# Attention with values of the narrow column groups multiplied in pairs, and a third buffer of probabilities

## The reference

```python
q, k, v = (to_heads(q), to_heads(k), to_heads(v))
dots = jnp.einsum('bhid,bhjd->bhij', q * scale, k)
causal = jnp.triu(jnp.ones((n, n), bool), k=1)
dots = jnp.where(causal, MASK_VAL, dots)
attn = jax.nn.softmax(dots, axis=-1)
out = jnp.einsum('bhij,bhjd->bhid', attn, v)
out = out.transpose(0, 2, 1, 3).reshape(b, n, d)
return out @ Wo.T + bo
```

```python
counts = jnp.bincount(a_e, length=E)
keep = counts <= cap
valid = keep[a_e]
```

## Time and profile before

| | |
|---|---|
| median of 3 runs | 1375.12 us (1373.54 to 1376.57) |
| profiled execution | 1374.71 us, span 1373.0 us |
| TensorE busy | 1273.9 us, 93% |
| VectorE busy | 1093.9 us, 80% |
| ScalarE busy | 942.2 us, 69% |
| GpSimd busy | 397.3 us, 29% |
| middle batch, 539.8 to 700.2 us | 160.4 us |
| granted TensorE clock, mean | 0.979 (1.00 from 120 to 1120 us) |
| DMA | 95.18 MB, mean 69 GB/s |

### The profile page before, as it was taken

One profiled execution on the slowest core, in us unless ns is written; L12 is line 12 of the kernel. 1 busy time (PEld: TensorE's weight loads), 2 busy tenths in 40 slices (PEclk: granted clock), 3 DMA queues, 4 the chain that ended last, 5 costly groups with the idle time before them and its releaser, 6 DMA issues.

```text
span 1373.0 us, 25088 instructions
## 1 busy us (share of the span) xinstructions
PE 1273.9 (93%) x8693; PEld 600.0 (44%) x8693; DVE 1093.9 (80%) x3527; ACT 942.2 (69%) x1697; POOL 397.3 (29%) x508
## 2 busy tenths in 40 slices
PE   6899999999999999999999999999999999999884
PEld 4433334444454444454444444544445544444332
DVE  6888888778887888878887788878888788779634
ACT  2257777777767777767767777677777677676752
POOL 3223322333232322332323332323222323222111
PEclk9889999999999999999999999999999999999977
DMA  4580443543325443324435423254442243340001
GB/s 134 114 156 13 70 70 58 100 75 74 68 37 100 90 70 70 61 63 89 70 59 101 83 62 68 40 101 89 70 70 53 38 92 70 58 69 32 1 1 34
DMA packets 57832, 95.18 MB, mean 69 GB/s; under 512 B 8352, under 2 KB 51488, under 8 KB 51744
## 3 DMA queue, kind: packets, MB, share of 16 engines
q1 hardware_dynamic: 55664, 92.30, 35.7%
q10 hardware_dynamic: 2032, 1.19, 0.3%
HBM read 59.91 MB, written 33.55 MB: 68 GB/s over the span
## 4 chain that ended last, share of the span: by engine, by line
PE 61%; DVE 21%; ACT 6%; issue 3%; DVEq 3%; DMA 2%; POOL 1%; SPq 1%; ACTq 0%; POOLq 0%
PE o_bank L1319 15%; PE s L1300 14%; PE st L1285 12%; DVE s L1011 8%; PE misc L1202 6%; PE misc L1186 4%; PE misc L1194 4%; DVE max_full L1015 3%; ACT probs L860 3%; PE misc L543 3%; DVE xn L519 2%; ACT q_stack L847 2%; DVEq L1022 2%; DVE stats L510 1%; DVE o_tok L1108 1%
## 5 line engine op out<-in xcount | busy, mean ns | idle before, releaser
L860 ACT ACTIVATE probs<-st 128x512 f32<-128x512 f32 (+1 forms) x1216 | 632.5, 581 | 192.2 <-PE st L1285 119.0
L1011 DVE CUSTOM_DVE_ANT_0 s<-s,causal 128x128 f32<-128x128 f32 (+3 forms) x1024 | 493.4, 502 | 131.9 <-PE s L1300 127.2
L1300 PE MATMUL s<-k_stack,q_stack 96*128 96x512 bf16 (+3 forms) x1536 | 493.7, 332 | 33.1 <-DVE max_full L1015 13.4
L1285 PE MATMUL st<-q_stack,k_stack 108*128 108x512 bf16 (+3 forms) x1536 | 486.8, 331 | 11.7 <-ACT probs L860 11.2
L1015 DVE TENSOR_REDUCE max_full<-s 128x1 f32<-128x512 f32 x512 | 349.7, 683 | 46.6 <-PE s L1300 46.3
L1319 PE MATMUL o_bank<-probs,v_aug 128*17 128x512 f32 (+3 forms) x3072 | 326.0, 496 | 5.4 <-POOL probs L734 5.2
L1300 PEld LDWEIGHTS s<-k_stack,q_stack 96*128 96x128 bf16 x1536 | 149.7, 98 | 373.1 <-DVE max_diag L1011 167.1
L734 POOL TENSOR_SCALAR_AFFINE_SELECT probs<-probs 128x512 f32<-128x512 f32 x256 | 163.5, 639 | 473.2 <-ACT probs L860 472.7
L1285 PEld LDWEIGHTS st<-q_stack,k_stack 108*128 108x128 bf16 x1536 | 149.8, 98 | 108.3 <-ACT probs L860 39.2
L746 POOL TENSOR_TENSOR qk<-qk,parts 128x512 f32<-128x512 f32 x64 | 75.0, 1171 | 282.4 <-ACT parts L820 282.4
L847 ACT ACTIVATE q_stack<-misc 12x2048 bf16<-12x2048 f32 x63 | 117.8, 1870 | 41.3 <-PE misc L1267 40.9
(11 more groups left out here) (115 smaller groups left out, 879.2 us busy)
## 6 DMA issues: line engine op xcount, KB each, us to landing
part_dram<-parts SPq DMA_DIRECT2D x128, 192.0 KB, 2.8
k_stack<-part_dram SPq DMA_DIRECT2D x186, 128.0 KB, 6.9
q_stack<-part_dram SPq DMA_DIRECT2D x31, 384.0 KB, 5.1
x_all<-x SPq DMA_DIRECT2D x16, 512.0 KB, 11.5
q_stack<-part_dram SPq DMA_DIRECT2D x31, 256.0 KB, 7.4
out<-x_all SPq DMA_DIRECT2D x7, 1024.0 KB, 10.6
q_stack<-part_dram SPq DMA_DIRECT2D x33, 128.0 KB, 9.0
k_stack<-part_dram SPq DMA_DIRECT2D x12, 64.0 KB, 3.0
```

The source lines that it names most:

```text
L860: nc.scalar.activation(probs[:, g % 2, h - part:h + 1, 0:width], st_bank[i % 3][:, 0:share * width] .rearrange("p (h c) -> p h c", c=width ...
L1011: nc.vector.tensor_tensor_reduce(out=bank, in0=bank, in1=causal[:, CW - width:CW], scale=1.0, scalar=-BIG, op0=ALU.add, op1=ALU.max, accum ...
L1285: score = nc.tensor.matmul(st_bank[i % 3][:, part * width:(part + 1) * width], k_stack[0:KROWS + MROWS, hg, h, jb * P:(jb + 1) * P], q_sta ...
L1300: nc.tensor.matmul(s_bank[u % 3][:, 0:width], q_stack[0:KROWS, hm, h, ib * P:(ib + 1) * P], k_stack[0:KROWS, hm, h, j0:j0 + width], start= ...
```

## The change

It does four things. The product with the values of every group stays behind unit (g + 2, 0), except groups 2 and 3, which both go behind the third score of group 4, unit (4, 2), one behind the other, and groups 10 and 11, which both go behind unit (0, 2) of the next head group. `probs` gets a third buffer, indexed g % 3 at the exponential, the selection and the product. The exponential of group g waits for one product less. And the scratch that is set aside for dynamic DMA descriptors is given as 8192 bytes, which makes room for the buffer.

```diff
+VALUES_BEHIND = {(g, 0): ((g - 2) % NGRP,) for g in range(NGRP) if g not in (0, 1, CT, CT + 1)}
+VALUES_BEHIND.update({(0, 2): (NGRP - 2, NGRP - 1), (CT, 2): (CT - 2, CT - 1)})
...
             plan.append(("st", g, h))
-            if h == 0 and not (hg == 0 and not prev and g < 2):
-
-                plan.append(("pv", (g - 2) % NGRP))
+            if not (hg == 0 and not prev and g < 2):
+                plan += [("pv", of) for of in VALUES_BEHIND.get((g, h), ())]
...
-        probs = sb("probs", [P, 2, HG, CW])
+        probs = sb("probs", [P, 3, HG, CW])
...
-                        now = probs[:, g % 2, :, 0:P]
+                        now = probs[:, g % 3, :, 0:P]
...
-                        wait(eng, sig.pv_done, lin(b, NGRP * NG, NGRP * hg + g - 1))
+                        wait(eng, sig.pv_done, lin(b, NGRP * NG, NGRP * hg + g - 2))
...
-                        nc.scalar.activation(probs[:, g % 2, h - part:h + 1, 0:width],
+                        nc.scalar.activation(probs[:, g % 3, h - part:h + 1, 0:width],
...
-                                                probs[:, g % 2, h, 0:CW - off], start=g in (0, CT),
+                                                probs[:, g % 3, h, 0:CW - off], start=g in (0, CT),
...
-    nc = bacc.Bacc("TRN2", target_bir_lowering=False, num_devices=1)
+    nc = bacc.Bacc("TRN2", target_bir_lowering=False, num_devices=1, dynamic_dma_scratch_size=8192)
```

## The result

| | before | after |
|---|---|---|
| median of 7 runs, us | 1374.01 (1372.94 to 1376.57) | 1382.09 (1379.13 to 1384.08) |
| ratio, 95% interval | | 1.0052 [1.0042, 1.0061] |
| span of the profiled execution, us | 1373.0 | 1380.4 |
| mean granted clock of TensorE | 0.979 | 0.978 |

A forecast was written before the change was run, and what follows sets the result against it. TensorE, 93% busy, but running into waits near most moved products. Places +9.4, batch 0 +1.0, last batch 0, selections -1.0 on 1374.7 gave 1384.1, said as 1384 us; own range 1379 to 1390, whole range 1366 to 1392.

The forecast's parts named there:

- covered slots: Where the 256-column product stands in a wait that doesn't move, removing it gains nothing; the place costs 0.44 us.
- the places: Eight places of a middle batch where products move: +1.57 us a batch, +9.4 us over six batches.
- term for the selections: Group 0's selection moves away from a VectorE cast, ends of head groups 1 and 2: -0.15 a batch, -1 in all.
- second rival: Cover is partly found again, evictions leave earlier and half the covers shift: no change, 1374 to 1377 us, chance 0.13.
- Seam and pair: All 63 pairs: no cost at the inner seam, next matmul 0.78 us after the pair starts, 0.21 us saved each.
- the prediction's sign: TensorE's waits for VectorE and ScalarE's copy grow by some 0.6 us in six of eight places of a batch.
- Head group 3, group 4: The next score waited for VectorE anyway, so moving the product costs +0.43 us here.
- The third buffer: ScalarE's 70.0 us of waits for products nearly vanish; worth 0 beyond the places, bounds 0 and -11.2 us.
- Batch 0 and the last batch: Batch 0 +1.0 us; in the last, two places' losses stand against about 0.6 us won: 0.
- A middle batch takes about 162 us: Sign that the forecast is right: a middle batch takes about 162 us instead of 160.4.
- all seams won: TensorE is the bound everywhere, 63 seams save 13.2 us: 1362 us; all or most seams won, chance 0.17.
- a seam that costs: Seam costs a full leave and entry, or a pair's second product waits for its selection: 1390 to 1397 us, chance 0.10.

The follow-up runs named there:

- filled kernel: Changed kernel plus twelve zero-weight matmuls in head group 3, where the 256-column product stood behind the first score of group 4: 1377.33 us, 1.0021 of the kernel before.
- narrow products: Kernel before, wide product over 1 column instead of 256 in covered places (group 2 in head groups 1 to 3, group 10 at their ends): 1377.80 us, 1.0032.
- pairs 2/3: Kernel before with the third buffer and only groups 2 and 3 paired, behind the third score of group 4: 1385.41 us, 1.0077.
- filled elsewhere: Changed kernel plus the same twelve zero-weight matmuls in head group 3, but behind the first score of group 8: 1387.21 us, 1.0089 of the kernel before.
- pairs late: Changed kernel with its pairs behind the first score of groups 5 and 1 instead of the third of groups 4 and 0: 1392.28 us, 1.0135 of the kernel before.
- buffer alone: Kernel before with third buffer, its indices, shorter exponential wait and smaller scratch; product order unchanged: 1371.98 us, 0.9984.
- pairs 10/11: Kernel before with the third buffer and only groups 10 and 11 paired, behind the third score of the next head group's group 0: 1367.72 us, 0.9944.
- both chosen ones: Kernel before, third buffer, groups 10 and 11 paired at ends of head groups 0 to 2, with or without 2/3 paired in head group 0: 1364.00, 1363.09 us.
- narrow open: Kernel before, product of group 6 over only its last 256 of 512 columns in every head group, an open place: 1366.52 us, 0.9944.

## Why the prediction was right, and where it was not

1384 us were forecast, 1382.09 measured, and a loss was forecast for a cause that the runs show, covered slots. That the total comes so near is in part luck. For the middle batches the forecast has +9.4 us from the places, some +8.5 with its term for the selections. Measured are +7.6: +4.1 from the places, -1.0 from the two-valued place below, which happened to be short in two batches more than before, and +4.4 from a clock that the forecast didn't think of. Without the clock's part the profiled execution would be near 1378 us (an estimate, 1382.1 - 4.4), and the filled kernel measures 1377.33: both under the forecast's own range of 1379 to 1390, and near the 1374 to 1377 of the second rival, for another reason than that rival's.

- **Seam and pair: right.** 58 of the 63 pairs are followed 0.77 or 0.78 us after their start, as forecast; four ran at 1.2 GHz (1.41 or 1.42 us), one had a wait behind it (1.12). The seam inside is 0. Of the two rules of the Trainium skill that the prediction weighed, this agrees with the one of TensorEngine Tiling (Array Packing), Key Properties, and not with the one on weight loads of TensorE: Matmul & The Clock Gate, Part 3, The mechanism: in the pair of 604.49 the loads of the second product start at 604.72, beside running matmuls of the first on the same rows, 0.21 us ahead of its own first matmul.
- **Covered slots: right.** +0.56, +0.27 and, at the end of head group 3, +0.43 stand against +0.54, +0.27 and +0.43. In batch 3 new waits of 0.40 to 0.55 us of TensorE stand in five of the eight places; the prediction's sign was some 0.6 us in six. That cover is the cause, and not the pair as such, is shown by the narrow products: 0.00 in the same places, without a pair.
- **Head group 3, group 4: mis-sized.** Before, this place takes 10.04 or 10.52 us, by which of two engines pays where a selection of GpSimd meets a VectorE operation (last section); the filled kernel takes 10.47 or 10.95. That is +0.43, as forecast, plus or minus a lottery of 0.48. On top came the clock, 1.3 to 1.6 us each time (11.78 and 12.03 against 10.47, 12.52 against 10.95), 4.4 us in all. The prediction didn't think of the clock.
- **Selections beside VectorE: mis-sized.** The term "I take -0.15 a batch" measured -0.26 and -0.37 in its two places: -0.63, or -3.8 us over six batches, inside its bounds of 0 and -6. The rows it rested on pointed there: the cast took 0.65 us beside the selection, 0.48 more than alone, and VectorE set the next start. At the end of head group 0 the cast fell as well, from 0.65 to 0.23 us; whether the -0.16 there is that, or the wait of 0.24 for the selection as forecast (-0.1), wasn't separated.
- **The third buffer: 0 forecast, -2.2 us measured.** Most of it, -0.22 us a batch, lies in head group 1, group 4, where the +0.54 was already read with the new exponentials; what the separate term of 0 missed is -0.06 a batch.
- **Batch 0 and the last batch:** +1.0 and 0 forecast, -0.2 and -0.5 measured, in part the same selections.
- **"A middle batch takes about 162 us": wrong by its own test.** Where the clock stays it takes 160.7 to 161.5 us (159.9 to 160.9 before), and 162.3 to 162.7 where it fell; the mean of the six is 161.7. A reader who checked only that number would have found it right for the wrong reason.
- The rivals: all seams won is excluded by the 0.00 of the narrow products; a partly found cover didn't occur; a seam that costs is excluded by the 0.78. No rival held what did happen, a clock that falls in an emptied slot, although the range did.

## What to carry to other kernels

Before work on the busiest engine is moved, look at what ends the wait in front of which it stands: if the next instruction starts when another engine is done, the work there is free, and moving it adds to the time wherever it lands with no wait behind (here 0.43 us for a 0.87 us pair, 0.27 where part of it met another wait). Move or merge only in places where the engine goes on with no wait behind. And give work that shares a port with a short operation on the path its own price: two selections moved away were worth 0.63 us a batch here, more than any other gain of the change.

## What the runs showed that I had not expected

**A short hole, in one place, and TensorE's clock at half.** With the slot of head group 3, group 4 empty, TensorE waits there for 0.60 to 0.75 us instead of 0.20 (two more waits, of 0.22 and 0.34 us, lie close by in all kernels), and in about half of the batches the clock falls to 1.2 GHz for 3.4 or 6.8 us. Count over the six middle batches of the one profiled execution of each kernel: with the slot empty in 16 of 30 (the change 3, pairs 2/3 3, filled elsewhere 3, pairs late 4, narrow 3), with the slot full in 1 of 42 (before, buffer alone, pairs 10/11, both chosen ones, filled slot, narrow open). In head group 0, group 4 of batch 0, where TensorE waits 0.86 us with the slot empty, it fell in four of six kernels with the slot empty and in none of six with it full; that counts for little, since in seven of the eight that kept it an earlier fall had ended a few us before. The other emptied slots, with waits of 0.51 to 0.54 us in group 4 of head groups 1 and 2 and of 0.40 at the ends of 1 and 3, never lost the clock in a middle batch. Why they didn't, and why one batch falls and the next, with the same rows, doesn't, stays open; so does whether a smaller filler would do. The Trainium skill (TensorE: Matmul & The Clock Gate, A second HAM failure mode: psum-queue depth-cycling) describes a clock that swings where the engine idles shortly between groups of matmuls; the 0.79 beside waits of 0.75 us agrees.

**One port, two durations.** Before, batches 1 and 3, the same VectorE operation and the same selection, 0.1 us apart in start:

```profile
357.25 0.40 DVE L519 TENSOR_SCALAR xn<-x_all,mean_var,rstd 128x256 f32<-128x256 f32 x1
357.35 0.81 POOL L734 TENSOR_SCALAR_AFFINE_SELECT probs<-probs 128x512 f32<-128x512 f32 x1 [1.43 <-ACT probs L860]
```
```profile
677.73 0.88 DVE L519 TENSOR_SCALAR xn<-x_all,mean_var,rstd 128x256 f32<-128x256 f32 x1
677.82 0.64 POOL L734 TENSOR_SCALAR_AFFINE_SELECT probs<-probs 128x512 f32<-128x512 f32 x1 [1.43 <-ACT probs L860]
```

Either VectorE takes 0.40 us and GpSimd 0.81, or 0.88 and 0.64. This is the lottery of 0.48 us above: in every middle batch in which the clock stayed, of all twelve kernels, the place is short with the first pair of times and long with the second. The Trainium skill (SBUF — State Buffer, Who interferes with whom) has the pair of ports that these engines share as an exclusive lock for a whole instruction. The trace agrees in that one of the two pays and not both. But what is paid, 0.17 or 0.48 us, is less than what was left of the other instruction (0.30 and 0.64), and VectorE starts first both times, so how long the lock is held and what decides between the two isn't shown here.
